# An LSTM cell inside a Mamba scan: three plain GpSimd operations on sigmoid values in place of four VectorE operations on tanh values; a third buffer for the products with B, and no hold of GpSimd

## The reference

```python
def step(h, inp):                      # Mamba, per channel c (256) and state n (16)
    dA = jnp.exp(dt_t[..., None] * A)
    h = dA * h + (dt_t * u_t)[..., None] * B_t[:, None, :]
    y = jnp.einsum('bcn,bn->bc', h, C_t)
...
g = xt @ wih.T + h @ whh.T + bih + bhh # LSTM, two directions of 64 units
i, f, gg, o = jnp.split(g, 4, axis=-1)
c = jax.nn.sigmoid(f) * c + jax.nn.sigmoid(i) * jnp.tanh(gg)
h = jax.nn.sigmoid(o) * jnp.tanh(c)
```

## Time and profile before

| | |
|---|---|
| median of 3 runs (lowest, highest) | 2159.1 us (2152.12, 2165.97) |
| span of the profiled execution | 2159.5 us |
| PE busy | 1857.5 us (86%) |
| DVE busy | 1645.7 us (76%) |
| ACT busy | 1298.3 us (60%) |
| POOL busy | 1011.2 us (47%) |
| stage of the scans | from 46 to about 838 us |

### The profile page before, as it was taken

How to read it: one execution, slowest core, us unless ns; L and a number is a source line. 1 busy time by engine, 2 the same in 40 slices (tenths; PEclk the granted TensorE clock), 3 DMA queues, 4 the chain that set the end, 5 groups by cost and what they waited for, 6 DMA issues and landing times. The chain is left out here.

```text
span 2159.5 us, 49411 instructions
## 1 busy us (share of the span) xinstructions
PE 1857.5 (86%) x19547; PEld 1357.8 (63%) x19547; DVE 1645.7 (76%) x2609; ACT 1298.3 (60%) x2660; POOL 1011.2 (47%) x775
## 2 busy tenths in 40 slices
PE   7888888889888867897878878889788699999999
PEld 4444444444443323444568877767676599999999
DVE  4999999999999996678465442346554589999897
ACT  5777777777776645114345444252456388888886
POOL 1777777777777773110017777300440033333333
PEclk9999999999999999899679999898899699999999
DMA  3544444444444442520038889501730411112000
GB/s 130 167 132 132 126 137 132 132 132 127 128 139 140 132 137 55 126 45 1 7 100 236 258 257 256 139 1 73 231 114 12 187 64 64 65 65 69 14 7 7
DMA packets 98037, 241.63 MB, mean 112 GB/s; under 512 B 15024, under 2 KB 48320, under 8 KB 95504
## 3 DMA queue, kind: packets, MB, share of 16 engines
q1 hardware_dynamic: 89120, 218.12, 32.7%
q0 software_dynamic: 7680, 15.74, 3.2%
q10 hardware_dynamic: 1008, 4.62, 0.6%
HBM read 226.25 MB, written 12.19 MB: 110 GB/s over the span
## 5 line engine op out<-in xcount | busy, mean ns | idle before, releaser
L1119 POOL TENSOR_TENSOR dBu<-du,Bs 128x858 f32<-128x858 f32 (+1 forms) x240 | 588.2, 2452 | 203.4 <-DVE hst L1046 94.6
L574 PE MATMUL py<-hst,ident 128*128 128x429 f32 (+1 forms) x960 | 416.7, 565 | 95.9 <-DVE hst L1056 95.1
L1046 DVE TENSOR_TENSOR_SCAN hst<-dA,dBu 128x858 f32<-128x858 f32 (+1 forms) x240 | 457.8, 1908 | 17.1 <-ACT dA L889 13.7
L889 ACT ACTIVATE dA<-dt,negA 128x416 f32<-128x416 f32 (+1 forms) x480 | 269.5, 596 | 177.2 <-DVE hst L1046 175.6
L574 PEld LDWEIGHTS py<-hst,ident 128*128 128x128 f32 x960 | 183.6, 202 | 292.3 <-DVE hst L1056 169.0
L3444 POOL TENSOR_TENSOR hm<-h,mw 128x264 f32<-128x264 f32 x128 | 89.7, 701 | 391.0 <-DVE h L3424 391.0
L1056 DVE TENSOR_TENSOR hst<-hst,Cs 128x858 f32<-128x858 f32 (+1 forms) x240 | 246.5, 1027 | 0.0
L3315 PE MATMUL pg<-hs,wh 128*128 128x66 f16 x6144 | 218.8, 194 | 4.8 <-issue 4.7
L3315 PE MATMUL pg<-xm,wi 128*128 128x66 f16 x6144 | 214.6, 195 | 6.8 <-issue 5.4
L3315 PEld LDWEIGHTS pg<-hs,wh 128*128 128x128 f16 x6144 | 204.8, 98 | 8.6 <-issue 5.1
L3315 PEld LDWEIGHTS pg<-xm,wi 128*128 128x128 f16 x6144 | 202.0, 98 | 11.3 <-issue 5.9
(11 more groups left out here) (568 smaller groups left out, 3458.8 us busy)
## 6 DMA issues: line engine op xcount, KB each, us to landing
wb<-sf_w SPq DMA_DIRECT2D x96, 514.0 KB, 4.9
Bs<-bc_rows SPq DMA_DIRECT2D x96, 429.0 KB, 4.6
Cs<-bc_rows SPq DMA_DIRECT2D x96, 429.0 KB, 3.5
mw<-route_weights SPq DMA_DIRECT2D x8, 2112.0 KB, 10.1
wb<-gf_w SPq DMA_DIRECT2D x24, 514.0 KB, 4.9
Bs<-bc_rows SPq DMA_DIRECT2D x24, 396.0 KB, 5.0
Cs<-bc_rows SPq DMA_DIRECT2D x24, 396.0 KB, 4.6
mb<-route_masks SPq DMA_DIRECT2D x8, 1088.0 KB, 5.8
```

The source lines that it names most:

```text
L574: return nc.tensor.matmul(out, weight, moving, **kw)
L889: last = a(o, by_seq(dt[:, j % 2, h, 0:n])[:, :, 1:S], ACT.Exp, scale=negA[:, l, h * DST + k:h * DST + k + 1])
L1046: v.tensor_tensor_scan(hst[:, g % HR, 0:2 * n], dA[:, g % 2, 0:2 * n], dBu[:, g % 2, 0:2 * n], 0.0, ALU.mult, ALU.add).then_inc(h_ready, 1)
L1119: g_.tensor_tensor(dBu[:, g % 2, 0:2 * n].rearrange("p (a n) -> p a n", a=2), du[:, j % 2, :, 0:n], Bs[:, q % NBS, k % BG, 0:n].unsqueeze( ...
```

## The change

The cell leaves VectorE. ScalarE now adds one more operation to `lstm_gates`: after the three tanh it turns all three into sigmoid values at once (0.5 x + 0.5, 192 columns, PSUM to SBUF, into `gates`), for which it waits for the tanh to be written. GpSimd makes one product of 128 columns (sigmoid(i) times the candidate beside sigmoid(f) times c), one sum of 64, and, one step later, one product of 64 for h. c and h are held as they are, so the halving of `whh` and `fw` goes, and `lstm_cell` has no scale. On GpSimd, `lstm_c` stands behind the product of k = 2, 6 and 10, and `lstm_h` behind that of k = 3, 7 and 11. dBu gets three buffers (DR = 3), so that GpSimd waits for scan g - 3 in place of g - 2. The wait at k = 10 goes. Two small fills are added ahead of the loops. The core of the diff:

```diff
+DR = 3
-        dBu = sb("dBu", [128, 2, 2 * SCW])
+        dBu = sb("dBu", [128, DR, 2 * SCW])
...
                 for g in range(3):
-                    a(act3[:, g, :], pre[:, g, :], ACT.Tanh, scale=0.5, bias=lb[:, 2, g:g + 1])
-                a(cz[:, 0, :], pre[:, 3, :], ACT.Tanh, bias=lb[:, 0, 3:4]).then_inc(gated, 1)
+                    last = a(act3[:, g, :], pre[:, g, :], ACT.Tanh, scale=0.5, bias=lb[:, 2, g:g + 1])
+                last.then_inc(tanhed, 1)
+                a(gc[:, 0, :], pre[:, 3, :], ACT.Tanh, bias=lb[:, 0, 3:4])
+                act.wait_ge(tanhed, t + 1)
+                a(gates[:, :, :], act3, ACT.Identity, scale=0.5, bias=half[:, :]).then_inc(gated, 1)
...
-            a(whh[:, :, :, :], whh[:, :, :, :], ACT.Copy, scale=0.5).then_inc(lw_ready, 1)
-            a(fw[:, 1, :], fw[:, 1, :], ACT.Copy, scale=0.5).then_inc(lw_ready, 1)
...
-                if j < LSTM_ITEMS:
-                    if k in (1 if j else 2, 5, 9):
-                        lstm_c(PER_ITEM * j + (k - 1) // 4)
-                    if k in (2 if j else 3, 6, 10):
-                        lstm_h(PER_ITEM * j + (k - 2) // 4)
...
+            def lstm_c(t):
+                pool.wait_ge(gated, t + 1)
...
+                g_.tensor_tensor(prod[:, :, :], gates[:, 0:2, :], gc[:, :, :], ALU.mult).then_inc(prods_ready, 1)
+                pool.wait_ge(prods_ready, t + 1)
+                if t >= 1:
+                    pool.wait_ge(tc_ready, t)
+                g_.tensor_tensor(gc[:, 1, :], prod[:, 0, :], prod[:, 1, :], ALU.add).then_inc(c_ready, 1)
+
+            def lstm_h(t):
+                pool.wait_ge(tc_ready, t + 1)
+                if t >= 2:
+                    pool.wait_ge(hs_kept, t - 1)
+                g_.tensor_tensor(hr[:, t % 2, :], gates[:, 2, :], tc[:, :], ALU.mult).then_inc(r_ready, 1)
...
-                if k == 10:
-                    if j + 1 < NI:
-                        pool.wait_ge(du_done, j + 2)
-                    if j >= 2:
-                        pool.wait_ge(m_scaled, j - 1)
...
-                if g >= 2:
-                    pool.wait_ge(h_ready, g - 1)
-                g_.tensor_tensor(dBu[:, g % 2, 0:2 * n].rearrange("p (a n) -> p a n", a=2), du[:, j % 2, :, 0:n],
+                if g >= DR:
+                    pool.wait_ge(h_ready, g - DR + 1)
+                g_.tensor_tensor(dBu[:, g % DR, 0:2 * n].rearrange("p (a n) -> p a n", a=2), du[:, j % 2, :, 0:n],
...
+                if j < LSTM_ITEMS and k in (2, 6, 10):
+                    lstm_c(PER_ITEM * j + (k - 2) // 4)
+                if j < LSTM_ITEMS and k in (3, 7, 11):
+                    lstm_h(PER_ITEM * j + (k - 3) // 4)
```

More of the change, by code:

```diff
@@ L476, in mamba_lstm @@
         fb = sb("fb", [128, 1])
-        cz = sb("cz", [128, 2, NB])
-        ig = sb("ig", [128, NB])
+        half = sb("half", [128, 1])
+        gates = sb("gates", [128, 3, NB])
+        gc = sb("gc", [128, 2, NB])
+        prod = sb("prod", [128, 2, NB])
         tc = sb("tc", [128, NB])
@@ L499, in mamba_lstm @@
             stage(nc, "wop_ready wop_kept cent_ready cent_kept sq_ready var_ready var_kept var_logged rstd_ready m_scaled m_done"))
-        (diag_ready, bias_set, lw_ready, gates_ready, gated, prods_ready, c_ready, tc_ready, r_ready, hs_kept, fused, fused_added) = ctx.enter_context(
-            stage(nc, "diag_ready bias_set lw_ready gates_ready gated prods_ready c_ready tc_ready r_ready hs_kept fused fused_added"))
+        (diag_ready, bias_set, lw_ready, gates_ready, half_set, c_zeroed, tanhed, gated, prods_ready, c_ready, tc_ready, r_ready, hs_kept, fused, fused_added) = ctx.enter_context(
+            stage(nc, "diag_ready bias_set lw_ready gates_ready half_set c_zeroed tanhed gated prods_ready c_ready tc_ready r_ready hs_kept fused fused_added"))
         b_loaded = ctx.enter_context(stage(nc, " ".join(f"b_loaded{k}" for k in range(NBS))))
@@ L676, in lstm @@
                     pe.wait_ge(l_loaded, 112)
-                    pe.wait_ge(lw_ready, 3)
                     pe.wait_ge(z_gated, 2)
@@ L865, in lstm_gates @@
                 for g in range(3):
-                    a(act3[:, g, :], pre[:, g, :], ACT.Tanh, scale=0.5, bias=lb[:, 2, g:g + 1])
-                a(cz[:, 0, :], pre[:, 3, :], ACT.Tanh, bias=lb[:, 0, 3:4]).then_inc(gated, 1)
+                    last = a(act3[:, g, :], pre[:, g, :], ACT.Tanh, scale=0.5, bias=lb[:, 2, g:g + 1])
[3 more added lines that the diff above has]
+                a(gates[:, :, :], act3, ACT.Identity, scale=0.5, bias=half[:, :]).then_inc(gated, 1)
             def lstm_cell(t):
                 act.wait_ge(c_ready, t + 1)
-                a(tc[:, :], cz[:, 1, :], ACT.Tanh, scale=0.5).then_inc(tc_ready, 1)
+                a(tc[:, :], gc[:, 1, :], ACT.Tanh).then_inc(tc_ready, 1)
             def lstm_keep(t):
@@ L920, in _ @@
             decay(2)
-            act.wait_ge(lw_ready, 3)
+            act.wait_ge(lw_ready, 1)
+            act.wait_ge(half_set, 1)
             lstm_gates(0)
@@ L977, in _ @@
             v.memset(dA[:, :, :], 0.0).then_inc(dA_zeroed, 1)
-            v.memset(cz[:, 1, :], 0.0)
             def soften(j):
@@ L1011, in back @@
                                        op0=ALU.mult, op1=ALU.mult).then_inc(m_scaled, 1)
[L1013 to L1031, removed]
             def fuse(c):
@@ L1045, in scan @@
                 dve.wait_ge(dA_ready, g + 1)
-                v.tensor_tensor_scan(hst[:, g % HR, 0:2 * n], dA[:, g % 2, 0:2 * n], dBu[:, g % 2, 0:2 * n], 0.0, ALU.mult,
+                v.tensor_tensor_scan(hst[:, g % HR, 0:2 * n], dA[:, g % 2, 0:2 * n], dBu[:, g % DR, 0:2 * n], 0.0, ALU.mult,
                                      ALU.add).then_inc(h_ready, 1)
@@ L1096, in build @@
                 g_.tensor_tensor(wt[:, l % 2, r, :], W(l, "wi", 0, DIN), cw[:, r, :], ALU.mult).then_inc(built, 1)
+            def lstm_c(t):
+                pool.wait_ge(gated, t + 1)
+                if t >= 1:
+                    pool.wait_ge(c_ready, t)
+                else:
+                    pool.wait_ge(c_zeroed, 1)
+                g_.tensor_tensor(prod[:, :, :], gates[:, 0:2, :], gc[:, :, :], ALU.mult).then_inc(prods_ready, 1)
+                pool.wait_ge(prods_ready, t + 1)
+                if t >= 1:
+                    pool.wait_ge(tc_ready, t)
[5 more added lines that the diff above has]
+                g_.tensor_tensor(hr[:, t % 2, :], gates[:, 2, :], tc[:, :], ALU.mult).then_inc(r_ready, 1)
             g_.memset(edge[:, 0:1], SER_B)
             g_.memset(edge[:, 1:2], 4000.0 / 32).then_inc(edge_set, 1)
+            g_.memset(half[:, :], 0.5).then_inc(half_set, 1)
+            g_.memset(gc[:, 1, :], 0.0).then_inc(c_zeroed, 1)
             g_.memset(whh[:, :, :, :], 0.0).then_inc(l_zeroed, 1)
```

## The result

The changed kernel takes 2191.1 us against 2161.9 in the runs beside it: ratio 1.014, 95% interval 1.0115 to 1.0165. The forecast was 2189 with 0.60 on slower. The profiled execution has a span of 2186.3 us (before 2159.5).

A forecast was written before the change was run, and what follows sets the result against it. VectorE was taken as the bound. From 2159 us, 11 items with cells at 2.3 us each (+25) and items 11 to 13 (+5) gave 2189 us. Range 2146 to 2222; the forecast's own, 2181 to 2215.

The forecast's parts named there:

- The bound and the turns: Scan stage: VectorE bounds; it and GpSimd alternate on the data path, a waiting product costing 1.6 us in `soften`.
- The cell leaves VectorE for 21.8 us: LSTM cells: 0.66 us each off VectorE's stream, 33 cells, 21.8 us, the whole possible gain.
- The hand-made item: One item with cells, timed: 5.5 us of blocked VectorE, item longer by 2.0 to 4.9, taken as 2.3.
- in plain steps nothing: Third dBu buffer: no gain in plain steps; its worth is that GpSimd may idle or be late without VectorE waiting.
- The ties, which I gave to VectorE: Product ending 0.07 us before the next weighing is issued: VectorE goes first; each tie GpSimd takes costs about 1.5 us.
- The 5 us forecast for items 11 to 13: Without the wait at k = 10, one product's turn in `soften` costs 1.6 us in each of three items: +5 us.
- GpSimd as the bound: Slower rival: GpSimd idles at k = 2, 6 and 10, each cell costing 3.0 us less 0.66: 2219 us, chance 0.15.
- The faster rival: GpSimd's extra 1.2 us a cell finds room and `soften` isn't broken into: 2145 us, or 2137 unblocked; chance 0.13.
- ScalarE's conversions: 33 sigmoid conversions of 0.35 us, 12 us beside 175.6 us of ScalarE idle: counted as nothing, at most 4 us.

The follow-up runs named there:

- two products: Kernel before, with two more full-width GpSimd products at k = 10 ahead of its wait there, written to unread tiles: ratio 1.0203, stage 837.0 us.
- ten cells beside the gate: Kernel before (two buffers, wait at k = 10 kept) with only the k = 2 cell on GpSimd in items 1 to 10: ratio 0.9952, median 2152.5 us.

## Why the prediction was right

*The bound and the turns.* Right, by the step itself. A product waiting behind a VectorE operation goes in front of the next one at 1.6 us (no hold alone: 23.0 us in 14 first operations; two products: +48.7 us). Items 11 to 13 are longer by 1.6, 1.7 and 1.4 us, as forecast, each with one operation of 2.6 to 2.7 us.

*The cell leaves VectorE for 21.8 us.* Right as far as it shows: ten cells beside the gate gave 7.1 us, 0.7 each, where I had 0.66. Its price on GpSimd, undisturbed, was 0.46 + 0.32 + 0.32 = 1.1 us where I had 1.2 from wider operations. The hand-made item had a cell at k = 6 cost 0.74 and 0.18 in weighings; with two buffers it is 0.64 and 0.25. But by itself the move gains 2.8 us, and my expectation for that run, a loss, was wrong: I had put into the cell what belongs to the third buffer.

*The third buffer, "in plain steps nothing", and its worth in letting GpSimd idle.* This is the step that failed. The third buffer alone costs 13.8 us where the hold stays. Nothing needed it: with two buffers VectorE waited 6.5 us for products. And it is the dearest part once the cells are on GpSimd: 785.5 to 812.8 with the hold, 799.3 to 820.0 without. With two buffers a product that is late is soon at its limit and starts when a scan ends, behind the weighing; with three it may start on its own, and since a product (1.71 us) is a little shorter than the free part of a step (1.77), it can end just before the next weighing is issued, and the following one gets in first. That both kernels with the cell and two buffers have no lost tie, and the changed kernel 11, is shown; that the 0.06 us between 1.71 and 1.77 decide is my reading of the order, and no run varied the product's length.

*The ties, which I gave to VectorE.* Wrong; GpSimd took 11 of them. I had 5.5 us blocked in an item with all ties to VectorE and 6.9 with one to GpSimd; the profile has 5.1 (34.7 us more in weighings and 20.9 more in the row, over 11 items). That the items came out 2.3 us longer, as forecast, is partly luck, since two errors stood against each other. The weighings lost 3.2 us an item where I had 1.9, by the ties. The row grew by 1.9 us where I had 3.7: it gave two full turns only in items 1 and 6 and one in the nine others, whose product of k = 10 was done before the row began, and the cell's small operations slip between VectorE's. Against the 5.1 stand the 2.0 of the cell and 0.8 of VectorE's idle time that went (18.1 us in items 0 to 10 before, 9.8 after), where I had 0.9.

*Hold.* Its removal costs 21.4 us in the kernel before and 7.2 in company of the other two parts, so the parts don't add. The 5 us forecast for items 11 to 13 came (4.7), but putting the hold back does not take them away, for with three buffers the lost tie takes their place.

*Rivals.* GpSimd as the bound (2219 us) needed waits of VectorE for products; there was one. The faster rival had a true core, that the cell at k = 2 finds room beside the gate; the version with that cell alone gains 7.1 us of the stage. ScalarE's conversions were free, as taken: waits for dA fell from 13.7 to 6.9 us.

What stays open: whether a shorter product or another order could avoid lost ties with three buffers and the cells on GpSimd wasn't tried.

## What to carry to other kernels

Where VectorE is the bound and works on two inputs in SBUF, a GpSimd operation that reads SBUF isn't free work beside it: look at whether VectorE operations last longer than their size says, since blocked time counts as busy. Let GpSimd start right after VectorE has started such an operation, and hold it ahead of a row of them; a further buffer takes that order away and can cost more than it gives. Moving the hold with it made that good where the cells stayed on VectorE (790.5 us), and not where they were on GpSimd (800.2 against 785.5 with two buffers). Put small work of GpSimd beside VectorE operations with an input in PSUM where there are any.

## What the runs showed of the hardware

- With operations waiting on both sides the data path changes hands after each operation: two waiting products block two successive VectorE operations (2.56 and 2.40 us in place of 1.04 and 1.12).
- A lead of 0.10 us at issue decides: the weighing at 733.03 waited for a product issued at 732.93 and took 2.82 us.
- Fills of 858 columns, 0.80 us each, neither block nor are blocked.
- Small GpSimd operations between two wide ones of VectorE cost it almost nothing, 0.04 us seen where one of 128 columns went in between (1.10 us against 1.06 undisturbed). Among the weighings, where they make a full product late, they cost more: 0.64 and 0.25 us on two weighings at k = 6.
